# Self-attention's small value matmuls put between the value matmuls of cross-attention, with the query projection moved to the fourth slot

## What is computed

```
x = x + xattn(layernorm(x), ctx, ctx, Wq, bq, Wk, bk, Wv, bv, Wo, bo)   # 16 heads of 16, softmax over 257 tokens
x = x + attn(layernorm(x), ...)                                         # 16 heads of 16 over the 32 tokens
x = x + ffn(layernorm(x), gate_w, gate_b, w1, b1, w2, b2)               # 8 experts, capacity 160

# attn, cut to what matters
q = rotary(rms_norm(x, qn) @ q_w.T + q_b);  k = rotary(rms_norm(x, kn) @ k_w.T + k_b);  v = x @ v_w.T + v_b
w = sigmoid(q @ k.T / 4);  w = w / (w.sum(-1) + 1e-8)
attn = (w @ v) @ o_w.T + o_b

# ffn, cut to what matters
expert = argmax(softmax(tokens @ gate_w + gate_b));  position = running count of the expert's tokens
out = gate_prob * (gelu(token @ w1[expert] + b1) @ w2[expert] + b2), where position < 160
```

## Time and profile before

| | |
|---|---|
| Median of the timed executions | 1329.99 us (1329.96 to 1330.12, 3 runs) |
| Profiled execution, its own time | 1326.77 us |
| Span of the profile, first to last instruction | 1324.9 us |
| TensorE busy with matmuls | 1160.6 us (88%), 17169 matmuls |
| Weight loads (PEld; they overlap matmuls) | 980.9 us (74%) |
| VectorE (DVE) | 851.6 us (64%) |
| ScalarE (ACT) | 801.9 us (61%) |
| GpSimd (POOL) | 568.9 us (43%) |
| Mean granted clock of TensorE over the span | 0.946 of full speed |

### The profile page before, as it was taken

How to read it: one execution, slowest core, us unless ns; L and a number is a source line. 1 busy time by engine, 2 the same in 40 slices (tenths; PEclk the granted TensorE clock), 3 DMA queues, 4 the chain that set the end, 5 groups by cost and what they waited for, 6 DMA issues and landing times. The chain is left out here.

```text
span 1324.9 us, 43348 instructions
## 1 busy us (share of the span) xinstructions
PE 1160.6 (88%) x17169; PEld 980.9 (74%) x17169; DVE 851.6 (64%) x2395; ACT 801.9 (61%) x2347; POOL 568.9 (43%) x1045
## 2 busy tenths in 40 slices
PE   6898988989889889999988988998999988874897
PEld 5677777777777777777777777777787777752796
DVE  4667777776776677766677766777666667653111
ACT  5677666666666666666666766766656666632121
POOL 2344444454554444445445444444444544432021
PEclk9999999998999999989999999999888999975899
DMA  6415111111111111111111111111111111000474
GB/s 156 124 46 182 54 58 54 58 57 34 52 50 54 49 36 50 51 47 52 36 47 48 50 51 31 50 50 51 46 45 36 48 50 46 14 10 13 135 227 138
DMA packets 71927, 82.32 MB, mean 62 GB/s; under 512 B 16987, under 2 KB 50732, under 8 KB 71728
## 3 DMA queue, kind: packets, MB, share of 16 engines
q1 hardware_dynamic: 65280, 75.19, 19.3%
q0 software_dynamic: 3200, 3.71, 0.8%
q10 hardware_dynamic: 3248, 0.66, 0.2%
HBM read 64.79 MB, written 16.56 MB: 61 GB/s over the span
## 5 line engine op out<-in xcount | busy, mean ns | idle before, releaser
L735 ACT ACTIVATE prob<-score,nmx 128x257 f32<-128x257 f32 x512 | 236.2, 476 | 219.1 <-DVE nmx L936 218.8
L401 PE MATMUL kps<-ctx_p,wk_p 128*128 128x256 f32 x1536 | 217.4, 292 | 0.3 <-POOL ctx_p L1235 0.2
L411 PE MATMUL vps<-wv_p,ctx_p 128*128 128x256 f32 x1536 | 214.7, 289 | 0.0
L401 PEld LDWEIGHTS kps<-ctx_p,wk_p 128*128 128x128 f32 x1536 | 200.0, 196 | 6.1 <-issue 1.9
L1235 POOL TENSOR_TENSOR ctx_p<-ctxT,ctx_p 128x512 fp32r<-128x512 f32 x128 | 152.3, 1190 | 117.1 <-ACT ctx_p L751 116.7
L411 PEld LDWEIGHTS vps<-wv_p,ctx_p 128*128 128x128 f32 x1536 | 191.5, 191 | 12.4 <-issue 12.4
L936 DVE TENSOR_REDUCE nmx<-score 128x2 f32<-128x514 f32 x256 | 165.2, 687 | 51.7 <-PE score L428 51.7
L1253 POOL TENSOR_TENSOR plast<-const,prob 128x128 f32<-128x128 f32 x128 | 64.1, 501 | 255.8 <-DVE prob L947 255.8
L947 DVE TENSOR_SCALAR prob<-prob,rsum 128x257 f32<-128x257 f32 x512 | 158.5, 352 | 9.0
L953 DVE COPY probT<-score 128x512 f32<-128x512 f32 x96 | 66.4, 691 | 126.2 <-PE score L444 125.9
L444 PE MATMUL score<-const,prob 128*128 128x128 f32 x1024 | 140.8, 281 | 2.3 <-DVE prob L947 2.1
(11 more groups left out here) (159 smaller groups left out, 2029.3 us busy)
## 6 DMA issues: line engine op xcount, KB each, us to landing
ctxT<-in_ctxT SPq DMA_DIRECT2D x128, 257.0 KB, 3.0
w<-in_w SPq DMA_DIRECT2D x16, 1024.0 KB, 8.7
xq<-in_x SPq DMA_DIRECT2D x32, 128.0 KB, 3.2
xr<-in_x SPq DMA_DIRECT2D x32, 128.0 KB, 2.1
qbd<-qkT SPq DMA_DIRECT2D x256, 16.0 KB, 1.9
out<-row SPq DMA_DIRECT2D x32, 128.0 KB, 1.9
slots<-row SPq DMA_DIRECT2D x10, 257.0 KB, 5.6
x_a<-slots SPq DMA_DIRECT2D x8, 129.0 KB, 2.1
```

Of the source, the lines that this page charges most:

```text
L401: last = mm(kps[:, c, :], wk_p[:, x, n, c * P:(c + 1) * P], ctx_p[:, g, y, n, :], start=(n, x) == (0, LO), stop=(n, y) == (C - 1, LO))
L411: last = mm(vps[:, c, :], ctx_p[:, g, x, n, c * P:(c + 1) * P], wv_p[:, y, n, :], start=(n, x) == (0, LO), stop=(n, y) == (C - 1, LO))
L735: last = af(prob[:, m, :], score[:, m, 0:S], ACT.Exp, bias=nmx[:, m:m + 1], scale=1.0, accum_out=esum[:, m:m + 1])
```

## The change

The heads of `self_values` are cut into a function of their own, `self_head`, and the waits into `self_ready`. In the second slot `values` waits for what the small matmuls need before it starts, and then issues one head (4 small matmuls, 8 with passes) behind each of its 12 matmuls. The last 4 heads are issued at place 3, behind the transposes. Where no value matmuls are left (the last two bodies), all 16 heads are issued at place 3.

Since both use `shared`, the query projection can no longer stand in the second slot. It goes to place 0 of the fourth slot, and ScalarE's `queries` goes to the start of ScalarE's fourth slot, before its exponentials. The row transposes and the gate move one place back, to places 1 and 2; the copy of the row transposes goes behind the copy of the keys on ScalarE, and `gate_exp` behind the copy of the transposed probabilities. The number of matmuls and copies is unchanged; no DMA and nothing on GpSimd, VectorE or SyncE is edited.

```diff
-            def values(t, j):
+            def values(t, j, aside=None):
                 b, g = TB * t + j, j % 2
                 pe.wait_ge(s["v_evac"], b)
+                if aside is not None:
+                    self_ready(aside)
                 for c in range(C):
                     for n in range(C):
-                        for x, y in PASSES:
+                        for at, (x, y) in enumerate(PASSES):
                             last = mm(vps[:, c, :], ctx_p[:, g, x, n, c * P:(c + 1) * P], wv_p[:, y, n, :],
                                       start=(n, x) == (0, LO), stop=(n, y) == (C - 1, LO))
-                last.then_inc(s["v_done"], 1)
+                            if (n, at) == (C - 1, len(PASSES) - 1) and c == C - 1:
+                                last.then_inc(s["v_done"], 1)
+                            if aside is not None:
+                                self_head((c * C + n) * len(PASSES) + at)
...
-            def self_values(t):
-
+            def self_ready(t):
+
+                turn("att2n_done", t + 1)
                 pe.wait_ge(s["sig_flat"], t + 1)
                 pe.wait_ge(s["v2_done"], t + 1)
                 if once(t):
                     pe.wait_ge(s["zeroed"], 2)
-                for h in range(H):
-                    for j in range(TB):
-                        rows = slice(32 * j, 32 * j + 32)
-                        last = mm(shared[rows, h * (HD + 1):(h + 1) * (HD + 1)], th[rows, h * L:(h + 1) * L], v2a[rows, h, :],
-                                  start=True, stop=True)
-                last.then_inc(s["pv2_ps"], 1)
+
+            def self_head(h):
+
+                for j in range(TB):
+                    rows = slice(32 * j, 32 * j + 32)
+                    last = mm(shared[rows, h * (HD + 1):(h + 1) * (HD + 1)], th[rows, h * L:(h + 1) * L], v2a[rows, h, :],
+                              start=True, stop=True)
+                if h == H - 1:
+                    last.then_inc(s["pv2_ps"], 1)
+
+            def self_values(t, beside):
+
+                if not beside:
+                    self_ready(t)
+                for h in range(C * C * len(PASSES) if beside else 0, H):
+                    self_head(h)
...
-                    (1, 0): q and (lambda: (turn("qT_done", i + 2), project_queries(i + 1))),
-                    (1, 2): s2 and (lambda: (turn("att2n_done", t2 + 1), self_values(t2))),
+                    (1, 3): s2 and (lambda: self_values(t2, xa)),
-                    (3, 0): s2 and (lambda: (turn("y2T_done", t2 + 1), transpose_rows(row, "y2_done", t2, "y2t_ps", sh_c))),
-                    (3, 1): s2 and (lambda: (turn("logit_done", t2 + 1), gate(t2))),
+                    (3, 0): q and (lambda: (turn("qT_done", i + 2), project_queries(i + 1))),
+                    (3, 1): s2 and (lambda: (turn("y2T_done", t2 + 1), transpose_rows(row, "y2_done", t2, "y2t_ps", sh_c))),
+                    (3, 2): s2 and (lambda: (turn("logit_done", t2 + 1), gate(t2))),
...
-                        values(ta, ja)
+                        values(ta, ja, t2 if j == 1 and s2 else None)
...
-                    if j == 3 and s2:
-                        copy_rows(y2T[:, :, :], sh_c, "y2t_ps", t2, "y2T_done")
+                    if j == 3 and q:
+                        queries(i + 1, 1 - half)
                     if xa:
                         exps(i, j)
-                    if j == 1 and q:
-                        queries(i + 1, 1 - half)
...
                     if j == 3 and s2:
-                        gate_exp(t2)
+                        copy_rows(y2T[:, :, :], sh_c, "y2t_ps", t2, "y2T_done")
                     if ahead:
                         values(ta, ja)
...
                     if xa:
                         probsT(i, j)
+                    if j == 3 and s2:
+                        gate_exp(t2)
```

## The result

The changed kernel takes **1490.62 us** (median of 4 executions, 1488.28 to 1491.22) where the kernel before took 1329.97 us beside it (4 executions). The ratio is **1.121, 95% interval 1.119 to 1.123**: slower by 161 us. The forecast was 1445 us, slower, in a range of 1360 to 1500 us.

A forecast was written before the change was run, and what follows sets the result against it. TensorE was taken as the main bound, busy 924 of 1022 us. Second slot +36, fourth slot +64 and clock +15 make +115 us on 1326.77, so 1442; the median's 3.2 us more gives 1445 us, range 1360 to 1500.

The forecast's parts named there:

- Second slot, switches: Second slot: twelve alternations with 32x32 tiles, 0.46 us a unit, make it 1.2 us longer per tile, +36 us.
- The 0.3 us in it for ScalarE's late copies: Second slot: ScalarE copies the stretched values later, delaying the context copy and its half of the probabilities, 0.3 us.
- Fourth slot: Fourth slot: moved projection and ScalarE's longer queue, with the gate's new wait, cost 2.2 us in 29 tiles, +64 us.
- values to gate: Fourth slot: after the values, the gate waits for ScalarE's row copy, a new wait of 1.35 us.
- The discount for VectorE's blocked product: Fourth slot, lower bound: a later place spares VectorE's 128x8 product 0.9 us, leaving 1.3 us a tile, +38 us.
- The clock: Loop: the clock falls in every tile at 1.2 us each, +15 us; bounds -21 and +50.
- At the price of the tile shown: Loop: each clock fall costs 36.94 - 35.75 = 1.2 us, from one period with a fall and one without.
- the prediction's own case: Whole kernel: 1400 to 1495 us, second slot 0.9 to 1.8, fourth 1.6 to 2.8 a tile, clock 0 to +30; 64 in 100.
- Free switching (1 and 2): Second slot: switching costs nothing and the clock stops falling; about 1333 us, 9 in 100, or 1306 us, 6 in 100.
- rival 2: Switching costs nothing and VectorE's blocked product passes ahead of GpSimd's work, only 1.3 us arriving: 1306 us, 6 in 100.
- The third: Second slot: switching costs as reckoned, but value matmuls in between keep the clock at 2.4 GHz; 1409 us, 15 in 100.
- The fourth: Whole kernel: every term at its upper bound, +54 + 90 + 50, above 1500 us; 6 in 100.

The follow-up runs named there:

- groups of two: Changed kernel with the twelve heads between value matmuls issued in six groups, two heads each, instead of one by one: 1346.46 us, ratio 1.017.
- e1: Changed kernel with all 16 heads as one block at place 2 of the second slot again, fourth-slot moves kept: 1353.43 us, ratio 1.021.
- e7: Changed kernel with twelve heads in three groups of four, and ScalarE's copy of the row transposes ahead of the keys' copy: 1303.34 us, ratio 0.984.
- e4: Changed kernel with one batch of four's self-value matmuls only, two small 32x32 matmuls behind each value matmul: 1507.93 us, one execution.
- e8: Changed kernel with each head replaced by two bf16 full-array matmuls of constants, 17 columns: 1325.21 us, one execution.
- three groups: Changed kernel with the twelve heads issued four at a time, behind the fourth, eighth and twelfth value matmul: 1322.2 us, ratio 0.996.
- e2: Kernel before with the whole self-value block moved from place 2 to place 3 of the second slot, behind the transposes: 1280.64 us, ratio 0.965.
- e9: Kernel before with the self-value block at place 3, and GpSimd's scatter moved behind the context tile's low part: 1279.62 us, ratio 0.963.

## Why the prediction came out as it did

The direction and the mechanism of both parts were right. Term by term, in the order of the prediction:

**Second slot, switches: right, slightly low.** A unit was to take 0.46 us and takes 0.49. The values start 2.84 us behind the scores (636.85 to 639.69), and 2.8 was worked out. For a second slot without a fall of the clock I take that of the groups of two, 9.04 us, and add what twelve units cost more than six double ones: 12 x 0.493 - (579.04 - 575.02) = 1.90. That is 10.94 us against 9.61 before at full clock: +1.33 us where 1.2 was written, +40 us in 30 tiles instead of +36. The 0.3 us in it for ScalarE's late copies do not show as a wait of TensorE; the units' 0.03 us, twelve times, took their place.

**Fourth slot: right.** 2.32 us instead of 2.2, 29 x 2.32 = +67 us instead of +64. The steps differ a little from the working: the exponentials come 1.54 us later (1.6), and by the starts, which is how the prediction reckoned, keys to row transposes take 0.34 us more than the 1.5 of their like (0.3 written), values to gate 1.22 (1.35). (The 0.18 and 1.05 us in the view's brackets count from the modelled ends.) That makes 0.92 + 0.34 + 1.22 - 0.33 = 2.15; the rest are lengthenings below 0.1 us each. The discount for VectorE's blocked product did not come. Groups of VectorE's instructions, kernel after:

```profile
L1095 DVE SCALAR_TENSOR_TENSOR eqr<-pr,row,const 128x8 f32<-128x8 f32 x32 | 29.0, 907 | 1.1
...
L1091 DVE TENSOR_SCALAR pr<-ex,rse 128x8 f32<-128x8 f32 x32 | 7.4, 230 | 1.1
```

The product `pr` of the earlier trace rows is short now, 230 ns where its mean was 932 before. But the next but one, `eqr`, went from 328 to 907 ns. In the tile shown GpSimd's low part of the context runs from 626.37 to 627.55 us and `eqr` from 626.60 to 627.57, so they end together, as that part and `pr` did before (222.69 and 222.71). The low part, which waits for ScalarE, came 2.56 us later behind the scores and VectorE's copy of the self values 2.29. So it meets another operation, which loses nearly as much: 0.58 us in the mean where `pr` lost 0.70. e1 and e7 show the fourth slot's term by itself and its largest step.

**The clock: the term that was mis-sized.** "The clock falls in every tile" holds for all 27 tiles. "At the price of the tile shown", 1.2 us, does not. The prediction let the fall begin behind the stretch, as it did behind the old block. It begins inside it, in the sixth to ninth unit, so the units behind that, the transposes, the last heads, the weighted values and in most tiles the start of the third slot run at 1.2 GHz. The price is 13.38 - 10.94 = 2.44 us in the second slot and 8.89 - 8.44 = 0.45 in the third: 2.9 us a tile. The kernel before lost 0.30 + 0.60 = 0.9 us in the same places (9.91 - 9.61 and 9.03 - 8.43, the latter its third slot at full clock). So the term is 30 x 2.0 = **+60 us, where +15 was written and +50 was the upper bound**. The length of the low stretches says the same. By the clock's record in the traces the loop of the kernel after is low for 8.0 us a tile; the kernel before was low for 2.5 us in the mean, and for 3.4 us in the tile whose price was taken. A microsecond at the low level costs 0.35 to 0.36 us in all three (2.9 / 8.0, 0.9 / 2.5, 1.2 / 3.4). So the price of low time was right, and how much of it a tile gets was not: 8.0 is more than twice 3.4, and twice as long was the prediction's upper bound. The step that failed is taking the price of a fall from a tile in which the whole block ran at full clock, for a stretch that I had just worked out to be twice as long.

Together 40 + 67 + 60, less 4 us in the first slot, is 163 us; the spans differ by 164.4 us. The time lies within the range, and even within the 1400 to 1495 us of the prediction's own case, though that case gave the clock +30 us at most. It does so because the other two terms came out near their middle and left room; for the clock this is luck.

**The rivals.** Free switching (1 and 2) is refuted by the 0.49 us of a unit, and by the distance between e4 and e8; the faster VectorE of rival 2 by the two groups above. The third, switches without a fall of the clock, holds for six and three groups but not for twelve: the groups of two are that case, 1346 us. The fourth, everything at its upper bound, came true for the clock alone. The thing not foreseen at all was on the side of the kernel before: its own block stood in the worst of the places tried, and moving it by one place is worth 3.5%.

**What stays open:** what the clock reacts to. Twelve trips through the 32x32 tiles lower it in every tile, and more with less work in them (e4); three or six trips, and twelve without a change of tile shape, leave it at 2.4 GHz in the 27 periods. Why the fall comes in the sixth to ninth unit and not earlier isn't told by these runs. That the missing 0.2 us a unit are a drain of TensorE is the reading that fits e4 and e8; the rows show the time and that no load begins ahead, not what the array does in it.

## What to carry to other kernels

Small matmuls in tiles of another shape are put beside large ones in groups, not one by one: what counts is the number of round trips, here 0.23 to 0.29 us each, and with twelve of them the clock fell in every tile. A block of small matmuls belongs where TensorE has to wait for another engine anyway; look for that place before cutting the block up. And when a step is moved into another slot, write down what the other engine's queue then does in order: the gate's new wait of 1 us was forecast from nothing but the copies that stand ahead of it in ScalarE's queue.

## What the runs showed of the hardware that was not expected

In the kernel before, the block of small matmuls stops twice, put down to issue, for 0.37 and 0.50 us. Timeline of TensorE, then of GpSimd, kernel before, the tile of the earlier trace rows:

```profile
602.88 0.56 PE L528 MATMUL shared<-v2a,th 32*32 32x17 f32 x45
603.81 0.26 PE L528 MATMUL shared<-v2a,th 32*32 32x17 f32 x6 [0.37 <-issue]
```

```profile
603.25 1.12 POOL L1311 DMA_INDIRECT slots<-row,sloti  x1 [0.86 <-ACT y1T L711]
```

The scatter's instruction runs on GpSimd from 603.25 to 604.37 us; the first stop begins at 603.26 and the block goes on for good at 604.57. In e1 the block starts earlier and stops behind 102 matmuls instead of 45, again where the scatter begins; in e2 the scatter starts 0.35 us ahead of the block and in most tiles one stop is left; with the scatter moved away (e9) the stops are gone in 26 of 27 tiles. Some tiles show it without any edit: in two of e1 the scatter starts only behind the block, in one of e2 it ends ahead of it, and in these three the block runs through in 1.08 us. So an indirect DMA issued by GpSimd held up the dense stream of small matmuls on TensorE. It is not the only thing that does: three tiles of e2 and one of e9 have a stop while no scatter runs. That it is the supply of instructions that runs dry meanwhile is only argued. In the kernel after, the scatter (also 1.12 us) falls into the alternation, and the units under it keep their 0.49 us. That nine matmuls in 0.49 us are too thin a stream to be stopped is a guess.
